# An audio block on one core: from 258-column halves with split operands to 512-token tiles with plain float32 products

## The reference, cut to what matters

```
zf, zi, zh = x@Wf+bf, x@Wi+bi, x@Wh+bh                       # mixer: a recurrence in logs
diff  = softplus(-zf) - softplus(-zi)
log_f, log_i = -softplus(diff), -softplus(-diff)
log_v = concat([log(0.5)], log_i + log_g(zh));  a = concat([0], log_f)
h = exp(a + cumlogsumexp(log_v - a))                          # 8 x 257 x 128: one position more

n = layernorm(h);  q, k, v = n@q_w.T, split(n@kv_w.T)         # 8 heads of 16
k, v = halves of the batch swapped                            # sample b reads k, v of b+4
h = h + softmax(q k.T / sqrt(128)) v

n = layernorm(h)                                              # FFN: shared + 16 experts of 96
y_e = (g*sigmoid(alpha_e g)*scale_e*(u+shift_e)) @ w2_e + b2_e,   g, u = clipped halves of n@w1_e + b1_e
h = h + y_shared + sum over the 2 best experts of weight_e * y_e
```

## Time and profile before

| | |
|---|---|
| median of 3 runs | 390.45 us (390.0 to 390.88) |
| span of the profiled execution | 388.2 us; it has no other time of its own |
| PE matmul busy | 316.8 us, 82%, 2160 instructions |
| DVE busy | 298.8 us, 77%, 500 |
| ACT busy | 243.1 us, 63%, 412 |
| POOL busy | 158.3 us, 41%, 125 |
| mean granted TensorE clock | 0.918 of 2.4 GHz |
| HBM read, written | 11.63 MB, 5.28 MB |

### The profile page before, as it was taken

The page is one execution under the profiler, slowest core; times in us unless marked ns, Lnnn a source line. Parts: engine busy times, 40 slices in busy tenths (PEclk is TensorE's granted clock), DMA queues, the critical chain, the costliest instruction groups (busy, mean ns, idle before and its releaser), DMA issues. The chain is left out here.

```text
span 388.2 us, 6049 instructions
## 1 busy us (share of the span) xinstructions
PE 316.8 (82%) x2160; PEld 258.7 (67%) x2160; DVE 298.8 (77%) x500; ACT 243.1 (63%) x412; POOL 158.3 (41%) x125
## 2 busy tenths in 40 slices
PE   3427028986968999999899999979999998879873
PEld 1105027854667878788588787968787887768752
DVE  7894646722579969978998999887976788887990
ACT  2684521542684858597598685675773877485751
POOL 1000372101032874744348577342234445357752
PEclk9767755798986999999999999989999999999998
DMA  7500850000390000008400000075000000000000
GB/s 270 221 0 0 220 80 2 0 3 0 117 183 0 2 3 1 0 3 218 56 28 2 2 3 0 2 207 67 28 2 0 3 2 0 0 31 3 0 1 27
DMA packets 12414, 17.30 MB, mean 45 GB/s; under 512 B 984, under 2 KB 9184, under 8 KB 12256
## 3 DMA queue, kind: packets, MB, share of 16 engines
q1 hardware_dynamic: 12384, 16.91, 17.6%
HBM read 11.63 MB, written 5.28 MB: 44 GB/s over the span
## 5 line engine op out<-in xcount | busy, mean ns | idle before, releaser
L506 POOL TENSOR_TENSOR te<-tbuf,ubuf 128x516 f32<-128x516 f32 x52 | 73.8, 1424 | 50.4 <-DVE tbuf L882 27.6
L956 PE MATMUL slot<-xh,w1h 128*128 128x258 f32 x208 | 64.7, 311 | 13.0 <-DVE xl L865 4.0
L495 POOL TENSOR_TENSOR ubuf<-ubuf,cwb 128x516 f32<-128x516 f32 x24 | 34.3, 1429 | 67.2 <-ACT cwb L659 48.9
L956 PE MATMUL slot<-xh,w1l 128*128 128x258 f32 x208 | 59.9, 288 | 0.0
L956 PE MATMUL slot<-xl,w1h 128*128 128x258 f32 x208 | 59.8, 288 | 0.0
L956 PE MATMUL slot<-te,w 128*128 128x258 f32 x208 | 50.7, 393 | 4.2 <-POOL te L506 3.5
L956 PEld LDWEIGHTS slot<-xh,w1h 128*128 128x128 f32 x208 | 40.3, 194 | 19.4 <-issue 14.0
L882 DVE SCALAR_TENSOR_TENSOR tbuf<-tbuf,gbuf 128x516 f32<-128x516 f32 x52 | 48.3, 935 | 6.0 <-ACT tbuf L666 5.6
L781 DVE TENSOR_REDUCE mx<-slot 128x2 f32<-128x514 f32 x64 | 41.6, 687 | 12.6 <-PE slot L956 12.4
L956 PEld LDWEIGHTS slot<-te,w 128*128 128x128 f32 x208 | 39.6, 195 | 12.8 <-POOL te L506 6.4
L646 ACT ACTIVATE gbuf<-slot,cst 128x516 f32<-128x516 f32 x52 | 35.8, 690 | 19.2 <-PE slot L956 16.8
(11 more groups left out here) (161 smaller groups left out, 614.6 us busy)
## 6 DMA issues: line engine op xcount, KB each, us to landing
qs<-spill SPq DMA_DIRECT2D x12, 258.0 KB, 4.5
ks<-spill SPq DMA_DIRECT2D x24, 129.0 KB, 5.9
spill<-qhl SPq DMA_DIRECT2D x4, 516.0 KB, 2.8
spill<-khl SPq DMA_DIRECT2D x4, 516.0 KB, 3.4
pt<-in_w SPq DMA_DIRECT2D x1, 1664.0 KB, 9.5
xt<-in_x SPq DMA_DIRECT2D x4, 256.0 KB, 5.4
out<-osb SPq DMA_DIRECT2D x8, 128.0 KB
te<-in_sel SPq DMA_DIRECT2D x1, 832.0 KB, 11.0
```

The costliest lines, as they stand in the source:

```text
L495: g.tensor_tensor(ubuf[:, c % NB, :, :], ubuf[:, c % NB, :, :], cwb[:, :, :], ALU.mult).then_inc(S["ucw"], 1)
L506: g.tensor_tensor(te[:, c % NTE, :, :], tbuf[:, c % NB, :, :], ubuf[:, c % NB, :, :], ALU.mult)\
L956: return nc.tensor.matmul(out_, lhsT, rhs, start=start, stop=stop, **k)
```

## The change

The kernel is written anew. What it does:

- *512-token tiles.* The first position, which is the same for all samples, leaves the tiles. A unit is [128, 512], one PSUM bank, one product. Its share in attention is the term `e0` = exp(-maximum) in the sum of the softmax (its score is 0 and its v is 0 after the norm, so the maxima are also cut at 0, `mz`). The output at the first position of all eight samples is made in a separate small pass (pieces beginning with z other than `z`: `zv` to `zstore`), with 8 columns a product.
- *Log mixer.* Everything is in logs: three log(1+exp(-|z|)) in one pass of 1536 columns (`e3`), sums by products with the identity and its negative into a PSUM bank (`lsum` 5, `wsum` 3, `wm` 1, `fsum` 3 products of 512 columns), scans from PSUM. No product passes on POOL but `dd` and `h1`.
- *32-row scores.* q and k stay in SBUF. A product takes the 32 rows of a pair of heads; one side is masked to each head in turn (`qm`, `km`), so one product of 512 columns gives the scores of two heads. `mx` for the maxima, `st` for the exponentials, with a second product that subtracts the maxima. 16 and 32 a unit. There is no trip to HBM.
- *Features by expert.* Partition 8e..8e+7 holds expert e in each of the first 12 chunks, chunk 13 is the shared expert. So one tile of weights (`cwb`) serves all 12, and clip bounds are a column for all.
- *Biases in weight rows.* The mean of a normed token is 0, so its first channel is the negative sum of the others: that row of w1 is subtracted from all others (`w1p`, on POOL, eight pieces) and its place holds the biases, with 1.0 in the normed tile (`one`).
- *One product per half.* `half_` is one plain float32 product of 512 columns; DVE clips straight from PSUM, but for the up halves of chunks 0 to 3, 6 and 7, which ACT copies and POOL clips. Chunks go on in pairs, 1024 columns an instruction (`th`, `gg`, `weigh`, `te`). `down` adds all 13 chunks and h (`y0`) in one bank.
- *Single banks, new orders.* Eight banks, given to each filling by a list (`BANK_OF`); new lists `AT`. SP loads w1 twice (the weights, and the row to subtract repeated over the partitions, 1.7 MB each), a `shift` row and w2. ACT's program waits for all constants before its first piece, and takes its clamps ahead of the mixer.
- Routing uses `max` and `match_replace` on [128, 4, 16]; the reciprocals of the softmax become log and exp on ACT (`den`).

The diff, cut:

```diff
+GATE_BY = ("V", "V", "V", "V", "V", "V", "V")
+UP_BY = ("AG", "AG", "V", "AG", "V", "V", "V")
+CW_BY = ("G", "G", "G", "G", "G", "G", "")
+TE_BY = ("G", "V", "G", "V", "G", "V", "V")
+NY, NV, NT = 3, 3, 4
+NPT = 4
...
-            def stack_q(st, u):
-                if u == 0:
-                    sp.wait_ge(s_zero, 1)
-                ge(sp, "h2n", 2 * u)
-                sp.wait_ge(S["spill_q"], 16 * (u + 1))
-                for r, src in enumerate((0, 1, 0)):
-                    sp.dma_start(qs[32 * r:32 * r + 32, :, :, :].bitcast(F32),
-                                 spill[u][src].rearrange("(t p) s n -> p s t n", p=32)).then_inc(S["stack"], 16)
...
+            def w1p(u, k):
+                pool.wait_ge(s_w1a, 16)
+                pool.wait_ge(s_w1b, 16)
+                step = (W1COLS + E) // W1_PARTS
+                cols = slice(k * step, (k + 1) * step)
+                g.tensor_tensor(w1[:, cols], w1[:, cols], w1_rows[:, cols], ALU.subtract).then_inc(s_w1, 1)
...
+            def weigh(u, k):
+                n = NP * u + k
+                clipped(pool, "u", UP_BY, n, "ucv", "ucg")
+                ps.released(pool, "cwb", u)
+                g.tensor_tensor(vr[:, n % NV, :, :], vr[:, n % NV, :, :],
+                                cwb[:, u % 2, :].unsqueeze(1).to_broadcast([P, 2, W]), ALU.mult).then_inc(S["vcg"], 1)
...
-            def up_half(st, u, c):
...
-                release(a(ubuf[:, c % NB, :, :], slot(st, ("u", c))[:, :, 0:W], ACT.Identity, bias=fpar[:, UB, c:c + 1]),
-                        st, ("u", c))
...
-            def clip_up(st, u, c):
-                released(dve, st, ("u", c))
-                p = c % NB
-                v.tensor_scalar(ubuf[:, p, :, :], ubuf[:, p, :, :], fpar[:, UHI, c:c + 1], fpar[:, ULO, c:c + 1],
-                                ALU.min, ALU.max).then_inc(S["uclip"], 1)
...
+            def e3(u):
                 tables(SET_EXP_LN)
+                for j in range(3):
+                    ps.released(act, "z", u, j)
+                ge(act, "wsum", u)
+                a(l3[:, :, :], z3[:, :, :], ACT.Exp, scale=-1.0).then_inc(S["e3"], 1)
+                ge(act, "e3", u + 1)
+                a(l3[:, :, :], l3[:, :, :], ACT.Ln, bias=one[:, :]).then_inc(S["l3"], 1)
...
+            def al_(u):
+                act.wait_ge(s_bias, BIASES)
+                ps.filled(act, "lsum", u)
+                if u:
+                    ps.filled(act, "fsum", u - 1)
+                z = ps.bank("lsum", u)[:, :]
+                a(al[:, :], z, ACT.Abs, bias=bias[:, CL:CL + 1]).then_inc(S["rl"], 1)
+                a(rl[:, :], z, ACT.Relu, bias=bias[:, CL:CL + 1]).then_inc(S["rl"], 1)
...
+            def et_(u):
+                ge(act, "wm", u + 1)
+                ge(act, "s", 2 * u)
+                last = a(et[:, :, :].rearrange("p s t -> p (s t)"), ps.bank("lsum", u)[:, :], ACT.Exp)
+                ps.release(last, "lsum", u)
...
+            def mscan(u):
...
+                    ps.filled(dve, "fsum", u - 1)
                 for s in range(2):
+                    v.tensor_tensor_scan(mrun[:, s, 1:N], ps.bank("lsum", u)[:, s * T:(s + 1) * T],
+                                         low[:, :].to_broadcast([P, T]), bias[:, NCL:NCL + 1], ALU.max, ALU.max)\
+                        .then_inc(S["m"], 1)
...
+            def mr(u, s, c, t):
...
+                last = v.tensor_reduce(mxt[:, s, c, 32 * t:32 * t + 2],
+                                       ps.bank("mx", u, s, c, t)[:, :].rearrange("p (i t) -> p i t", i=2), AX_X, ALU.max)
+                ps.release(last, "mx", u, s, c, t)
...
+            def gate_evict(u, c):
+                n = NP * u + c // 2
+                ps.filled(dve, "g", u, c)
+                dve.wait_ge(s_par, PARS)
+                ge(dve, "gg", n - NY + 1)
+                r = col(c)
+                last = v.tensor_scalar(yr[:, n % NY, c % 2, :], ps.bank("g", u, c)[:, :], fpar[:, GHI, r:r + 1],
+                                       fpar[:, GLO, r:r + 1], ALU.min, ALU.max)
+                ps.release(last, "g", u, c)
...
-            def max_(st, u, s, c, t):
...
-                take(pe, st, name)
-                for i in range(2):
-                    last = mm(slot(st, name)[:, i, 0:W], qs[0:KR, s, t, c * P:(c + 1) * P], ks[0:KR, 1 - s, t, i, :])
-                fill(last, st, name)
-            def half_(st, u, c, k):
...
-                take(pe, st, name)
-                for s in range(2):
-                    o = slot(st, name)[:, s, 0:W]
-                    mm(o, w1h[:, k, c, :], xh[:, s, :], stop=False)
-                    mm(o, w1h[:, k, c, :], xl[:, s, :], start=False, stop=False)
-                    last = mm(o, w1l[:, k, c, :], xh[:, s, :], start=False)
-                fill(last, st, name)
...
+            def lsum(u):
+                ps.take(pe, "lsum", u)
+                if u == 0:
+                    pe.wait_ge(s_bias, BIASES)
+                    pe.wait_ge(s_second, 16)
+                o = ps.bank("lsum", u)[:, :]
+                mm(o, wd[:, :], xt[:, u, :], stop=False)
+                ps.released(pe, "z", u, 0)
+                ps.released(pe, "z", u, 1)
+                mm(o, hident, z3[:, 0, :], start=False, stop=False)
+                mm(o, nhident, z3[:, 1, :], start=False, stop=False)
+                ge(pe, "l3", u + 1)
+                mm(o, ident, l3[:, 0, :], start=False, stop=False)
+                ps.fill(mm(o, nident, l3[:, 1, :], start=False, stop=True), "lsum", u)
+            def wsum(u):
+                ge(pe, "rl", 2 * u + 2)
+                ge(pe, "lp", u + 1)
+                o = ps.bank("lsum", u)[:, :]
+                mm(o, ident, rh[:, :], start=False, stop=False, skip_group_check=True)
+                mm(o, nident, z3[:, 2, :], start=False, stop=False, skip_group_check=True)
+                mm(o, nident, l3[:, 2, :], start=False, stop=True, skip_group_check=True).then_inc(S["wsum"], 1)
+            def wm(u):
+                ge(pe, "m", 2 * u + 2)
+                o = ps.bank("lsum", u)[:, :]
+                mm(o, nident, mrun[:, :, 1:N], start=False, stop=True, skip_group_check=True).then_inc(S["wm"], 1)
+            def fsum(u):
+                ps.take(pe, "fsum", u)
+                ge(pe, "m", 2 * u + 2)
+                ge(pe, "ll", u + 1)
+                o = ps.bank("fsum", u)[:, :]
+                mm(o, ident, mrun[:, :, 1:N], stop=False)
+                mm(o, nident, rl[:, :], start=False, stop=False)
+                ps.fill(mm(o, nident, al[:, :], start=False, stop=True), "fsum", u)
+            def mx(u, s, c, h):
+                ps.released(pe, "q", u)
+                ge(pe, "km", 2 * u + 2)
+                for t in (2 * h, 2 * h + 1):
+                    ps.take(pe, "mx", u, s, c, t)
+                for t in (2 * h, 2 * h + 1):
+                    rows = slice(32 * t, 32 * t + 32)
+                    ps.fill(mm(ps.bank("mx", u, s, c, t)[:, :], qt[rows, s, c * P:(c + 1) * P],
+                               km[rows, 1 - s, :, :].rearrange("p i t -> p (i t)")), "mx", u, s, c, t)
+            def st(u, s, c, h):
+                ge(pe, "qm", 2 * u + 2)
+                ps.released(pe, "k", u)
+                for t in (2 * h, 2 * h + 1):
+                    ps.take(pe, "st", u, s, c, t)
+                for t in (2 * h, 2 * h + 1):
+                    rows = slice(32 * t, 32 * t + 32)
+                    mm(ps.bank("st", u, s, c, t)[:, :], kt[rows, 1 - s, c * P:(c + 1) * P],
+                       qm[rows, s, :, :].rearrange("p i t -> p (i t)"), stop=False)
                 ge(pe, "nm", 2 * u + s + 1)
+                for t in (2 * h, 2 * h + 1):
+                    rows = slice(32 * t, 32 * t + 32)
+                    ps.fill(mm(ps.bank("st", u, s, c, t)[:, :], const("onesr")[rows, :],
+                               nm[rows, s, :, :].rearrange("p i t -> p (i t)"), start=False, stop=True), "st", u, s, c, t)
+            def pv(u, s, c):
+                n = 4 * u + 2 * s + c
+                ps.released(pe, "st", u, s, c, PAIRS - 1)
+                ps.released(pe, "v", u)
+                o = ps.bank("o0", u, s)
                 ones32 = const("ones32")
+                for half in range(2):
+                    for i in range(2):
+                        for t in range(PAIRS):
+                            lhsT = ones32[:, 32 * i:32 * i + 32] if half else vpad[:, 2 * (1 - s) + c, t, i, :]
+                            last = mm(o[32 * t:32 * t + 32, half * T:(half + 1) * T], lhsT, pt[:, n % NPT, 2 * t + i, :],
+                                      start=False, stop=(c == 1 and i == 1), skip_group_check=True)
+                last.then_inc(S["pv"], 1)
+            def half_(u, c, name, kind):
+                ge(pe, "one", u + 1)
+                pe.wait_ge(s_w1, W1_SET)
+                ps.take(pe, name, u, c)
+                ps.fill(mm(ps.bank(name, u, c)[:, :], w1_of(c, kind), xn2[:, u % 2, :]), name, u, c)
...
+            def down(u, k):
```

(63 more changed lines are left out.)

1580 lines of the change are left out of this document (787 added, 793 removed), and 116 rows, old and new, of tables (AT, BANK_OF, BY, ENGINES).

## The result

The changed kernel takes 412.52 us (median of 4 runs, 409.17 to 414.59), the kernel before on the same chip 390.66: ratio 1.055, 95% interval [1.050, 1.061]. It is slower by 5.5%; I had forecast 357 us and a range of 330 to 390. The profiled execution took 409.17 us over a span of 407.4.

The account below looks back on a forecast made before the run. DVE was nearest to a bound, the head second; PE would become the bound at 310 us. Head 99 + PE queue 229 + changes 8 + waits 13 + end 6 = 355 us span, forecast 357, range 330 to 390.

Parts of the forecast that it names:

- What moved: Whole kernel: the bound moves to PE at 310 us, with DVE 210 to 225, ACT 188, POOL 140.
- the spill's wait: Head: PE's 14.15 us wait for k to come back from HBM, forecast to fall away with the HBM trip.
- The head: Up to the first FFN product: scores begin at 42 or 46, first FFN product due at 99 us, against 108.7.
- Scores: ... four abreast they are 12 products, 10.3 us: Scores on PE, per unit: 16 mx and 32 st products on 32 rows, four abreast, cost 10.3 us.
- the changes: PE's 84 switches between full, 32-row and 32-column products; 55 behind the head at 0.15 us, 8 us (bounds 0 and 22).
- My own sign of being wrong: Forecast is wrong if mx and st exceed 15 us of PE a unit, or certain PE waits total over 30 us.
- Four 301 us ... the pass 9 us: PE's work: 75.2 us a unit, four 301 us, plus 9 us for the eight first positions' pass: 310 us.
- Waits: PE's waits behind the first FFN product: 5 to 6%, 13 us (bounds 0 and 47); waits for maxima before it, 5.
- The rival "pairs": Scores: mx and st run two abreast, 41 us more, 13 replacing waits: 385; shares chance 0.23 with waits as now.
- The rival "row groups one after another": Scores: products on different row groups don't overlap, 124 us more, 16 absorbed by waits: 465; chance 0.05.
- That side: Slower than before, chance 0.12: serial row groups 0.05, pairs and waits together (395 to 405 us) 0.07.

## Why the prediction was wrong

- **What moved** was right: DVE 226.5 (210 to 225 forecast, so just above), ACT 180.0 (188), POOL 144.4 (140), 16 table loads, halves' instructions 0.43 apart, the spill's wait gone. Clips from PSUM took 803 ns, not 690, without harm: DVE waits for PE.
- **The head** was right to the first score (49.6, forecast 46). From there to the first FFN product I had 53 us, and it took 64: that stretch holds 12 of the 33 runs of scores.
- **"Scores: ... four abreast they are 12 products, 10.3 us"** is the step that failed. 41.2 us became 72.7. That row groups overlap, four deep, was right. What I priced was one endless run with all banks free. PE's order cuts the 192 products into 33 runs, and a run lasts at least 0.86 us for each product that stands on its fullest row group (the 32 rows that most of its products use), a turn, plus 0.2 at its ends. That is 62 turns where I had 48 (12.0 us more) and 6.6 us of ends, which I had among the changes. The remaining 12.9 us are pairs that start late, after their banks. Nine runs are of two products (1.06 us each), nine of eight, eight of which take 2.8 to 3.1 us instead of 1.9. I had the order in front of me and counted its changes, but did not count how many products stand between two of them. My own sign of being wrong, over 15 us a unit, came true: 18.2.
- **"Four 301 us ... the pass 9 us"** for full and 32-column products, with 8 us for changes. Full products were forecast at 241 and took 269.3. Of the 28, some 9 are instructions at half clock (those of 512 columns 0.85 us apart, most past 360, where the windows show 0.80). Of 496 instructions of 512 columns 371 are 0.43 apart and 86 between 0.5 and 0.6: about 6 us of it stands at changes, about 6 more between products of the same kind. A change costs 0.2 at each side, not 0.15, so 84 cost 17 us with those in the head, which I had left out. What is left of the 28 I did not separate. The halves alone took 97 us for a forecast of 89; the kernel before has 85 for them, where the prediction reckoned 75 at full clock.
- **Waits** were right in sum: 25.3, with the start and the end 35, against 37 in the forecast. Up to the first FFN product they were 16 with the start (forecast 18), behind it 15 (forecast 13), of which 10.4 lie past 360 us, and after PE's last instruction 4 of the 6 that I had for the end.
- **The rival "pairs"** named the place and nearly the size (41 us more; 31 measured). Its mechanism, banks that come free one by one, is 12.9 of the 31; short runs are the rest, so that its total came near is partly luck. I let waits absorb 13 us of it, which they did not.
- **The rival "row groups one after another"** named the number that decides, 1.9 abreast. It was 2.27 (165 / 72.7), and the kernel is slower all the same, since full products were 28 us dearer too. That side had 0.12, and nothing past 405 had a chance of its own: errors of the sum all add on the engine that is full, and I had let them cancel.
- **Orders.** I gave no term to their quality. Another order of PE alone is worth 21 us, as much as the whole loss.

So the change traded time on engines that overlap (DVE, ACT) and waits for time on the one that was then full: 12 mixer products a unit (41 us), halves at 0.858 for three parts (97 us against 85), and the scores (73 us against 61).

## What to carry to other kernels

Price products on part of the array by the run in which they stand, not by the best rate: list the runs between two changes, take the fullest row group times one product's time, add 0.2 for a run's ends. Then ask when each bank comes free: a pair whose bank is late runs behind its neighbour, and waiting for all four banks gains nothing. When one engine becomes the bound, every small error of its sum adds to the time, so its sum needs a range of its own and the forecast one upward. And try its order before its work: moving 21 of 308 pieces brought 5%, more than taking 20 products off it in the wrong stage (0.6%).

## What the hardware showed

- PE's clock fell while only a part of the array worked, not only where PE waited. In the kernel with products alone, behind full products at 2.4 GHz, single and paired 32-row products came down to 1.2 GHz though PE was busy all through (window, PE busy, clock, DMA share, GB/s):

```profile
25.95:35.34 9.39, 9.33 (x16) 0.75 0.00 0
35.34:49.43 14.09, 14.02 (x32) 0.50 0.01 1
...
57.51:64.83 7.32, 7.25 (x64) 1.00 0.00 0
```

- Products on free row groups start ahead of earlier ones that wait for their rows. In the run at 137.52 above the issue order is pair, subtraction, pair, subtraction, and all four products (x8) started before the first subtraction; the second pair started 0.03 us behind the first.
- A multiplication of 512 columns in SBUF by a column took 0.42 us before. In the new kernel one mask had a mean of 1.32 us and the one beside it 0.70:

```profile
L812 DVE TENSOR_SCALAR qm<-qt,cst 128x512 f32<-128x512 f32 x8 | 10.3, 1322 | 9.9 <-PE bank L1038 9.9
...
L818 DVE TENSOR_SCALAR km<-kt,cst 128x512 f32<-128x512 f32 x8 | 5.3, 699 | 0.2
```

  The trace shows why they differ. With POOL idle each took 0.47 to 0.49 us. Five of the sixteen ran while a POOL instruction with tensors in SBUF was already under way, took 1.23 to 3.93 us, and ended 0.28 to 0.29 us after it. One of them, and the mask behind it:

```profile
138.52 3.27 POOL L496 TENSOR_TENSOR vr<-vr,cwb 128x1024 f32<-128x1024 f32 x1 [3.74 <-DVE vr L900]
139.77 2.31 DVE L812 TENSOR_SCALAR qm<-qt,cst 128x512 f32<-128x512 f32 x1 [0.20 <-PE bank L1038]
142.00 0.47 DVE L818 TENSOR_SCALAR km<-kt,cst 128x512 f32<-128x512 f32 x1
```

- 1664 additions on one partition cost POOL 3.88 us, as much as 3.3 passes of 128x418 (1.17 us each).
